# Plain norms one step later on ScalarE, the tile maximum ahead of the plain pairs on VectorE, scores through memory head by head

## The reference

```python
# layer 2: messages over the edges, summed per source node, then per node
os1 = ssp(s_in @ w_f2o1_s / sqrt(2F));  ov1 = v_in @ w_f2o1_v / sqrt(2F)
os2 = os1 @ w_f2o2_s / sqrt(B);         ov2 = ov1 @ w_f2o2_v / sqrt(B)
x = layernorm(x + concat(os2, ov2))
# layer 3: attention over the edges, 8 heads of 64, W is 512 x 1536
q, k, v = split(x @ W);  aw = sum_f(q[src] * k[dst])            # (edges, 8)
m = segment_max(aw, src);  e = exp(aw - m[src]);  alpha = e / segment_sum(e, src)[src]
x = layernorm(x + segment_sum(alpha * v[dst], src))
```

## Time and profile before

| | us |
|---|---|
| median of 3 runs | 2432.24 |
| lowest and highest run | 2429.86, 2434.51 |
| the profiled execution, whole | 2433.44 |
| its span in the trace | 2431.7 |
| PE busy in the span | 1893.0 (78%) |
| DVE busy | 1588.0 (65%) |
| ACT busy | 1057.3 (43%) |
| POOL busy | 945.2 (39%) |

### The profile page before, as it was taken

One profiled execution on the slowest core, in us unless ns is written; L12 is line 12 of the kernel. 1 busy time (PEld: TensorE's weight loads), 2 busy tenths in 40 slices (PEclk: granted clock), 3 DMA queues, 4 the chain that ended last, 5 costly groups with the idle time before them and its releaser, 6 DMA issues. The chain is left out here.

```text
span 2431.7 us, 23979 instructions
## 1 busy us (share of the span) xinstructions
PE 1893.0 (78%) x5496; PEld 939.5 (39%) x5496; DVE 1588.0 (65%) x2664; ACT 1057.3 (43%) x2019; POOL 945.2 (39%) x1055
## 2 busy tenths in 40 slices
PE   5999995999999999999998492255378887888400
PEld 2444442444444444444444241133244444444200
DVE  5464551677777777777775051799467787777864
ACT  2343442455555555555554131244355544454222
POOL 2211111566666565666665633465211111111124
PEclk9999997999999999999999796555579998899755
DMA  7732124444444444444443734333533433434433
GB/s 263 246 117 56 18 26 90 144 145 157 153 151 159 143 165 143 161 148 156 154 148 112 212 44 75 94 87 78 192 131 123 160 131 130 176 129 148 165 123 109
DMA packets 152093, 326.07 MB, mean 134 GB/s; under 512 B 21969, under 2 KB 35186, under 8 KB 151766
## 3 DMA queue, kind: packets, MB, share of 16 engines
q1 hardware_dynamic: 120518, 244.22, 29.0%
q0 software_dynamic: 28160, 76.53, 12.7%
q10 hardware_dynamic: 3344, 4.51, 0.6%
HBM read 185.35 MB, written 139.84 MB: 134 GB/s over the span
## 5 line engine op out<-in xcount | busy, mean ns | idle before, releaser
L661 PE MATMUL d_p_h<-w3a,d_xT 128*128 128x512 f32 x640 | 290.5, 597 | 25.3 <-DMA d_xT<-in_xT 25.3
L661 PE MATMUL d_p_o<-d_w,d_uT 128*128 128x512 f32 x640 | 291.1, 598 | 3.0 <-ACT d_uT L736 3.0
L661 PE MATMUL d_p_p<-d_wr,d_x1T 128*128 128x512 f32 x640 | 290.4, 597 | 0.0
L818 DVE TENSOR_TENSOR d_zz<-d_yg,d_xbeta 128x512 f32<-128x512 f32 x80 | 138.5, 1732 | 98.8 <-POOL d_yg L869 98.8
L550 POOL TENSOR_SCALAR d_small<-d_mv 128x1 f32<-128x1 f32 x160 | 81.8, 512 | 306.3 <-DVE d_mv L787 156.4
L661 PEld LDWEIGHTS d_p_h<-w3a,d_xT 128*128 128x128 f32 x640 | 122.6, 192 | 180.8 <-issue 180.8
L661 PEld LDWEIGHTS d_p_o<-d_w,d_uT 128*128 128x128 f32 x640 | 122.3, 192 | 157.4 <-issue 152.8
L1482 POOL DMA_INDIRECT f_sums<-sum,index x40 | 44.4, 1110 | 323.3 <-PE f_p_T L1518 312.2
L729 ACT ACTIVATE d_yn<-d_y,d_small 128x512 f32<-128x512 f32 x80 | 65.1, 814 | 231.9 <-POOL d_small L555 231.9
L661 PEld LDWEIGHTS d_p_p<-d_wr,d_x1T 128*128 128x128 f32 x640 | 116.6, 192 | 116.9 <-issue 116.9
L282 PE MATMUL m_p_H<-m_xT,m_w 128*128 128x512 f32 x320 | 146.9, 613 | 4.8 <-ACT m_xT L323 4.8
(11 more groups left out here) (250 smaller groups left out, 4215.8 us busy)
## 6 DMA issues: line engine op xcount, KB each, us to landing
state<-d_empty SPq DMA_DIRECT2D x80, 264.0 KB, 2.1
sum<-m_tile_sum SPq DMA_DIRECT2D x10, 2048.0 KB
d_xT<-in_xT SPq DMA_DIRECT2D x80, 256.0 KB
d_z<-sum SPq DMA_DIRECT2D x80, 256.0 KB
d_x<-in_x SPq DMA_DIRECT2D x80, 256.0 KB
x<-d_x SPq DMA_DIRECT2D x80, 256.0 KB
p<-d_p SPq DMA_DIRECT2D x80, 256.0 KB
pair_p<-p SPq DMA_DIRECT2D x40, 512.0 KB
```

What stands on the lines that cost most here:

```text
L661: last = nc.tensor.matmul(out[:, :], lhsT[:, c, :], w[:, c, :], start=(c == 0), stop=(c == KB - 1))
L818: nc.vector.tensor_tensor(zz[b][:, :], yg[b][:, :], xbeta[b][:, :], ALU.add).then_inc(zz_done, 1)
```

## The change

1. `plain_plan` becomes 3, 3, 2, 2 and then 2 and 1 in turn, over 24 steps instead of 25. Even steps from 4 on carry two pairs and odd ones one, as before; steps 1 and 3 get one pair more, and step 24 with its two pairs is gone.
2. ACT: the norms of a step's pairs are taken in the step after. All but one of them (or the one, if there is one) stand after the copies of the turned sums, ahead of `query_out`; where there are several the last stands at the end of the step. `away_from` goes to the start of the step, `state_factors` ahead of the second `second_product_out`, `weights` ahead of `x3_rows`.
3. DVE: `merge` stands between the two `moments`, and `tile_maximum` ahead of the plain pair. `pair_leaky` comes before `weigh_values` and `pair_moments` after it; a second pair stays at the end of the step.
4. Scores: the store to memory is laid out head by head (`(h p)` in place of `(p h)`), so that it writes single elements of 4 bytes, 1024 of them, where it wrote 128 rows of 32 bytes. The load is as large as before and contiguous as before, and DVE reads `spread` in order (line 1768) where it read with a stride of 8 elements.
5. SP: in steps that follow a step with three pairs, loads and stores stand ahead of the scores; in the others all loads stand ahead of all stores.

```diff
 def plain_plan(steps):
-    plan = [3, 2, 2] + [1 + i % 2 for i in range(steps - 3)]
+    plan = [3, 3, 2, 2] + [2 - i % 2 for i in range(steps - 4)]
     assert sum(plan) == PAIRS
     return plan
...
     with phase(nc, "f_") as (sb, ps, sem), ExitStack() as ctx:
-        T, AHEAD, STEPS = EDGE_TILES, 6, EDGE_TILES + 5
+        T, AHEAD, STEPS = EDGE_TILES, 6, EDGE_TILES + 4
         w1s, w1v, w2s, w2v = sb("w1s", [2 * F, B]), sb("w1v", [2 * F, B]), sb("w2s", [B, B]), sb("w2v", [B, B])
         sums = [sb(f"sums{i}", [P, 8 * F]) for i in range(AHEAD)]
         sumT = [sb(f"sumT{i}", [2 * F, 4, P]) for i in range(2)]
...
         neg, rstd, shift = ([sb(f"{n}{i}", [P, 2]) for i in range(2)] for n in ("neg", "rstd", "shift"))
         slots = lambda first, n: k.same_dst[:, first:first + n, :].rearrange("p t e -> p (t e)")
-        spread, prod, q = slots(0, 8).rearrange("p (e h) -> p e h", h=HEADS), slots(8, KB), slots(12, KB)
+        spread, prod, q = slots(0, 8).rearrange("p (h e) -> p h e", h=HEADS), slots(8, KB), slots(12, KB)
         srcT = k.same_dst[:, 16:20, :]
         dstT = [k.column_acc[:, i, :].rearrange("p (c e) -> p c e", c=KB) for i in range(2)]
         cand = k.filters[:, :, :, :].rearrange("p t c f -> p (t c f)")[:, KB * 2 * D:KB * 2 * D + HEADS * P].rearrange(
...
             sp.dma_start(k.wv[:, :, :], k.L3_W[:, 2 * D:3 * D].rearrange("(c p) n -> p c n", p=P)).then_inc(k.wqk_in, 16)
             pair = 0
             for step in range(STEPS):
+                here = HERE[step - 1] if step else 0
+                if here > 2:
+                    for j in range(pair, pair + here):
+                        pair_load(nc, k, sp, j + 2)
+                        pair_store(nc, k, sp, j)
                 t = step - 3
                 if 0 <= t < T:
                     sp.wait_ge(aw_done, t + 1)
-                    sp.dma_start(k.aw_rows[t, :].rearrange("(p h) -> p h", h=HEADS), k.scores[:, t, :]
+                    sp.dma_start(k.aw_rows[t, :].rearrange("(h p) -> p h", h=HEADS), k.scores[:, t, :]
                                  ).then_inc(aw_out, 16)
                     sp.wait_ge(aw_out, 16 * (t + 1))
                     if t:
                         sp.wait_ge(cand_done, t)
-                    sp.dma_start(spread[:, :, :].rearrange("p e h -> p (e h)"),
+                    sp.dma_start(spread[:, :, :].rearrange("p h e -> p (h e)"),
                                  k.aw_rows[t:t + 1, :].to_broadcast([P, P * HEADS])).then_inc(spread_in, 16)
-                for _ in range(HERE[step - 1] if step else 0):
-                    if pair + 2 < PAIRS:
-                        pair_load(nc, k, sp, pair + 2)
-                    pair_store(nc, k, sp, pair)
-                    pair += 1
+                if here <= 2:
+                    for j in range(pair, pair + here):
+                        if j + 2 < PAIRS:
+                            pair_load(nc, k, sp, j + 2)
+                    for j in range(pair, pair + here):
+                        pair_store(nc, k, sp, j)
+                pair += here
             while pair < PAIRS:
                 pair_store(nc, k, sp, pair)
                 pair += 1
...
             nc.scalar.preload_act_table_set(ACT_SET)
             pair = 0
-            for step in range(STEPS):
+            for step in range(STEPS + 1):
                 a, b, c, d, e = step, step - 1, step - 2, step - 3, step - 4
+                late = HERE[step - 1] if step else 0
+                if 0 <= d < T:
+                    away_from(d)
                 if 0 <= b < T:
                     second_product_out(b, 0)
                 if 0 <= c < T:
                     x3_turned_out(c, 0)
                     x3_turned_out(c, 1)
+                if 0 <= e < T:
+                    state_factors(e)
                 if 0 <= b < T:
                     second_product_out(b, 1)
                 if a < T:
                     sums_turned_out(a, 0)
-                if 0 <= e < T:
-                    state_factors(e)
-                if 0 <= d < T:
-                    away_from(d)
+                for _ in range(max(late - 1, min(late, 1))):
+                    pair_normalise(nc, k, act, pair)
+                    pair += 1
                 if 0 <= c < T:
                     query_out(c)
                 if a < T:
                     first_product_out(a, 0)
                     sums_turned_out(a, 1)
+                if 0 <= d < T:
+                    weights(d)
                 if 0 <= b < T:
                     x3_rows(b)
-                if 0 <= d < T:
-                    weights(d)
                 if a < T:
                     first_product_out(a, 1)
                     logarithms(a)
-                for _ in range(HERE[step]):
+                if late > 1:
                     pair_normalise(nc, k, act, pair)
                     pair += 1
...
                 dve.wait_ge(away_done, t + 1)
                 if t:
                     dve.wait_ge(top_done, t)
-                nc.vector.tensor_tensor(cand[:, :, :], spread[:, :, :].rearrange("p e h -> p h e"),
+                nc.vector.tensor_tensor(cand[:, :, :], spread[:, :, :],
                                         away[:, :].rearrange("p (a e) -> p a e", a=1).to_broadcast([P, HEADS, P]),
                                         ALU.add).then_inc(cand_done, 1)
                 dve.wait_ge(cand_done, t + 1)
...
                     new_maximum(e)
                 if 0 <= b < T:
                     moments(b, 0)
-                    moments(b, 1)
                 if 0 <= e < T:
                     merge(e)
-                extra = HERE[step]
-                if extra:
-                    pair_leaky(nc, k, dve, pair)
-                    if extra == 1:
-                        pair_moments(nc, k, dve, pair)
-                        pair += 1
+                if 0 <= b < T:
+                    moments(b, 1)
                 if 0 <= d < T:
                     tile_maximum(d)
-                if extra > 1:
-                    pair_moments(nc, k, dve, pair)
-                    pair += 1
+                if HERE[step]:
+                    pair_leaky(nc, k, dve, pair)
                 if 0 <= d < T:
                     weigh_values(d)
+                if HERE[step]:
+                    pair_moments(nc, k, dve, pair)
                 if a < T:
                     softplus(a)
-                for _ in range(extra - 1):
-                    pair_leaky(nc, k, dve, pair)
-                    pair_moments(nc, k, dve, pair)
-                    pair += 1
+                for j in range(pair + 1, pair + HERE[step]):
+                    pair_leaky(nc, k, dve, j)
+                    pair_moments(nc, k, dve, j)
+                pair += HERE[step]
```

## The result

The changed kernel is slower: a median of 2556.0 us over 4 runs (2549.85 to 2560.03) against 2433.38 us for the kernel before beside it (4 runs, 2429.86 to 2436.48). The ratio is 1.0502, with a 95% interval of 1.0473 to 1.0531. The forecast was 2364 us with a range up to 2410, so both the sign and the range were wrong. The profiled execution took 2559.03 us, its span is 2557.3.

What follows compares the result with a forecast made beforehand. The loop was taken to be bound by hand-overs, through ACT's late copy `f_y`. Gains of 50.4 us in 8 periods and 18.8 at the end, less 0.8 in front, made 68.4: 2365.0 profiled, 2364 median, range 2338 to 2410.

Steps and rivals of the forecast that it cites:

- What bounds the kernel: In the 16-step loop no engine is full; hand-overs bind it, at 51.0 us per period of two steps.
- The hand-over through `f_y`: At even steps' end ACT waits 5.35 us for DVE's second pair, so `f_y` comes late and PE idles 6.74 us.
- Rival 1: In even steps PE keeps its full clock; period 43.1 us, 15 us less in all, 2350 us; chance 0.12.
- Part 1: Norms one step later on ACT: its 5.35 us wait goes, no work added, buffer delay taken at nothing.
- Rival 2: The two pair buffers bind: `pair_moments` waits for stores, some 4 us a period, 2400 us; chance 0.12.
- Part 2: DVE reads `spread` in order at line 1768: 1.22 us instead of 2.01, 15.8 us of DVE time in all.
- the forecast's own walk: The new loop steps summed operation by operation: odd step 25.1 us, even step 19.6.
- Part 3: Scores stored head by head from SP's queue: 1.0 us more taken, between bounds of 0.5 and 9.9.
- rival 3: The single-element store delays the tile maximum: 20 us per us beyond 1.0, less 10; up to 2532 us; chance 0.10.
- Part 4: Tile maximum ahead of the pair: in odd steps DVE newly waits for `spread`, landing 7.3 us after the scores start.
- the forecast's own period: One odd and one even loop step: 44.7 us instead of 51.0, 50.4 us gained in 8 periods.
- Part 5: The plan moves two pairs from step 24 into steps 1 and 3: front loses 0.8 us, end gains 18.8.

Runs made afterwards that it cites:

- e1_rows: The changed kernel with scores stored as 128 rows of 32 bytes and read with the stride, as before; 2366.92 us, ratio 0.9773 to the kernel before.
- e9_x3_first: e4_norms_late with ACT taking `x3_rows` ahead of `weights` again, as in the kernel before; 2431.49 us, ratio 0.9999 to the kernel before.
- e4_norms_late: e1_rows with DVE's order of work as in the kernel before; 2463.88 us, ratio 1.0156 to the kernel before.
- e6_turned: The changed kernel with scores turned on DVE in 32x32 blocks and stored as 128-byte pieces by four transfers; 2388.59 us, ratio 0.9827 to the kernel before.
- e3_probe: The kernel before with small awaited transfers of up to 1024 pieces added behind its last phase; own time not compared, 1024 neighbouring elements cost 9.1 to 10.3 us.
- e2_heads_only: The kernel before with only the scores' new layout, stored head by head and read in order; 2539.41 us, ratio 1.0471 to the kernel before.
- e11_odd_only: e1_rows with the odd step's pair loaded a step earlier and its `pair_leaky` ahead of the tile maximum; 2393.43 us, ratio 0.9834 to the kernel before.

## Why the prediction was wrong, point by point

**What bounds the kernel** was read rightly. The hand-over through `f_y` went as forecast: PE's wait is gone in the changed kernel and in e1_rows. That it alone was worth the time was not so: in e9_x3_first it is gone as well (0.8 us once), and the time is that of the kernel before. Rival 1, PE at its full clock in even steps, did not come. PE's records of the same operation in an odd and an even step of e1_rows, at granted clocks of 1.00 and 0.50:

```profile
2022.44 1.02 PE L1555 MATMUL f_p_R<-src_rows_sb,ident 128*128 128x512 f32 x2
...
2047.29 2.07 PE L1555 MATMUL f_p_R<-src_rows_sb,ident 128*128 128x512 f32 x2 [2.77 <-DVE f_outT L1748]
```

**Part 1, the norms.** No work added, the delay of the buffers covered: in e1_rows DVE waits for stores of pairs 1.9 us in 400. The cover that the prediction named, the tile work, is the right one, as e4_norms_late shows by taking it away (42.6 us of waits for loads and stores). Rival 2 did not come.

**Part 2, the read in order.** The price was right, 1.23 us against the 1.22 taken. The 15.8 us are DVE's time and not a gain: in the forecast's own walk the fast read is worth only some 0.5 us a period, because with it the pair's load comes last in odd steps and PE's values in even ones. In e6_turned, the one kernel with the fast read and a fast store, no gain over e1_rows is left.

**Part 3, the store, is the step that failed.** It took 1.0 us for a term that the bounds put between 0.5 and 9.9; measured, from store to load, 11.24 us less 1.41, 9.8 us more. That the upper bound comes so close is luck: it let the price grow with the number of pieces, and in e3_probe 256 elements already cost 7.6 us. The reason given, "most of 1.41 us cannot be packet time when the packets fill 0.08 of it", is true and decides nothing: packet time was never what grew. In e3_probe the packets are through 1.6 us after the issue and the wait ends 8.6 us later. With rows only for 128 pieces of 32 bytes, nothing in the trace of before could tell between the two ends, and the choice should have stayed open: rival 3 held the mechanism and the place, its break-even was 4.9 us more, half of what came, and I gave it 0.10. What the prediction made of the 512-byte rule of the Trainium skill (DMA: Bandwidth & Descriptors, Specifications), a sum that stays the same to 0.2 us a tile, is refuted with it: 32-byte rows and 4-byte elements both lie under that rule and cost 1.4 and 10 us. That the 64 packets of its section Bandwidth are those of one engine was my reading; the section does not say so. Another line of the Trainium skill, on the same page (DMA: Bandwidth & Descriptors, Rules for kernel authors) names a non-contiguous last dimension as one descriptor per element, to be avoided; the measured direction agrees with it.

**Part 4, the new wait.** From scores to maximum the sum was 6.27 + 1.0. Its second term had a smaller fault of the same kind: the load's 3.43 us were taken to the end of its packets. From the load's issue to the maximum e1_rows takes 2035.60 - 2031.24 = 4.36 us, the changed kernel 5.00 (2085.87 - 2080.87) and 5.68, and over all its 20 tiles 4.3 to 6.5. So of 17.7 us, 1.4 are scores, 11.2 the store and 5.0 the load. The rows of e1_rows behind this:

```profile
2031.24 0.32 SPq L1468 DMA_DIRECT2D same_dst<-aw_rows  x1
...
2035.60 2.02 DVE L1779 TENSOR_TENSOR filters<-same_dst,f_away 128x1024 f32<-128x1024 f32 x1 [1.66 <-DMA same_dst<-aw_rows]
```

Put into the forecast's own period, with (17.7 - 7.3) + (18.6 - 7.3) - 1.05 of slack = 20.7 more, it gives 65.4; measured 64.3.

**Part 5, the plan, and the steps.** Without the slow store the plan held: in e1_rows the front takes 0.1 us less than before (forecast 0.8 more) and the end 17.0 less (18.8). The 16 steps take 42.3 us less, where the forecast had 50.4. Walked again with the old read and the old store, the odd step takes 24.3 us and the even one 19.9, a period of 44.2 and 54 us less; e1_rows takes 45.7 a period. So this part of the sum, too, promised 12 us too much. The load's term above is 0.9 of the 1.5 us a period; for the rest there is DVE's wait of 0.90 us for ACT's factors in the even step at 2053.55, which the walk did not have. In all it is 59.4 us of phase against 68.4. In the changed kernel the same three are 8.0 more, 106.5 more and 9.9 more.

**The whole.** The profiled execution is 194.0 us above the forecast's 2365.0: 7.2 in the front, 156.9 in the 16 steps, 28.7 at the end, 1.2 outside the phase. Rival 3's rule, 20 us for each us of the store less 10, gives 166 for 8.8 us more, 2530; for the other 26 the load's term, 0.9 to 3.1 us more than 3.43 in each of 20 steps, is more than enough. All of the change but its item 4 was worth 2.3%; item 4, a layout of 4 KB in memory, cost 1.0502 / 0.9773, 7.5%.

## What to carry to other kernels

A transfer that an engine waits for is priced from issue to landing, never from its packets, and a store whose neighbouring elements come from different partitions has no price until it has been measured: keep 16 bytes or more of each partition together, even if that leaves a strided read behind. When a reordering takes the cover away from a transfer, any unknown in that transfer's price stands on the critical path once a step, and the chance of the rival must be as wide as the bounds of the price. Parts of a reordering can be worth nothing alone and 2% together, so undoing them one at a time doesn't give their shares.

## What the runs showed of the hardware that I had not expected

- 128 elements of 4 bytes from 128 partitions, stored side by side, land after 7.1 us; at a pitch of 8 bytes after 3.1, at 16 bytes and more after 1.4 (once 2.0). Pieces of 16 bytes or more without gaps land after 1.4 to 1.9 us.
- The price grows with the count at first and then hardly: 1.3 us for 16 elements, 2.9 for 32, 6.7 for 64, 7.1 for 128, 7.6 for 256, 9.3 to 10.8 for 512, 9.1 to 10.3 for 1024. Reading 1024 such elements takes 2.1 to 2.4 us.
- The packets of such a store of 1024 elements are on record within 1.6 us of its issue, 8.6 us before the wait for it ends, so packet time is not what a waiting engine sees. The record of the landing is: in e2_heads_only it says 9.5 to 11.1 us from issue (median 10.7 of 20), and SP's next issue follows at once.
- A 4 KB store issued right behind 1 MB of loads in the same queue took 4.1 to 5.6 us instead of 1.4 (e11_odd_only).
